# Last stage of a four-layer token tower: the weighted sum of gathered rows on VectorE in place of ScalarE and one reduction

## The reference

```
q = (x @ Wq).reshape(b, n, HEADS, DIM) * DIM ** (-0.5)
kv_scores, indices = _pk(x, Wq_pk, pk_keys)
offsets = jnp.arange(HEADS) * NUM_KV
ind = indices + offsets[None, None, :, None]
k = jnp.einsum('bnhk,bnhkd->bnhd', kv_scores, keys_table[ind])
v = jnp.einsum('bnhk,bnhkd->bnhd', kv_scores, values_table[ind])
sim = jnp.einsum('bihd,bjhd->bhij', q, k)
...
attn = jax.nn.softmax(sim, axis=-1)
out = jnp.einsum('bhij,bjhd->bhid', attn, v)
return out @ Wo
```

## Time and profile before

| what | us |
|---|---|
| median of three runs | 12374.88 |
| profiled execution, own time | 12427.32 |
| its span, first to last instruction | 12425.6 |
| PE busy | 9322.9 |
| DVE busy | 8840.9 |
| ACT busy | 6949.5 |
| POOL busy | 6941.6 |
| first gather of the last stage starts | 5385.5 |
| last maximum (L2966) starts | 12382.7 |

### The profile page before, as it was taken

How to read it: one execution, slowest core, us unless ns; L and a number is a source line. 1 busy time by engine, 2 the same in 40 slices (tenths; PEclk the granted TensorE clock), 3 DMA queues, 4 the chain that set the end, 5 groups by cost and what they waited for, 6 DMA issues and landing times.

```text
span 12425.6 us, 139805 instructions
## 1 busy us (share of the span) xinstructions
PE 9322.9 (75%) x38094; PEld 4917.2 (40%) x38094; DVE 8840.9 (71%) x23183; ACT 6949.5 (56%) x15135; POOL 6941.6 (56%) x5848
## 2 busy tenths in 40 slices
PE   1565667566745656359989989898999889898987
PEld 1251222222213113225545545454555445554545
DVE  3633899789983884777777777777777777777762
ACT  0211544354431002148777877788788778777784
POOL 3000777577750000057777777777777777777671
PEclk9955788778875777579999999999999999999996
DMA  0000333233320000022222222222222222222220
GB/s 20 8 17 3 113 119 124 82 116 119 126 75 11 14 7 9 1 58 64 60 65 60 67 57 63 59 63 59 61 64 58 64 56 65 58 64 60 61 58 19
DMA packets 538617, 723.65 MB, mean 58 GB/s; under 512 B 412866, under 2 KB 420593, under 8 KB 503386
## 3 DMA queue, kind: packets, MB, share of 16 engines
q0 software_dynamic: 168448, 338.54, 10.2%
q1 hardware_dynamic: 369418, 376.55, 9.8%
HBM read 697.87 MB, written 8.42 MB: 57 GB/s over the span
## 4 chain that ended last, share of the span: by engine, by line
PE 32%; DVE 10%; ACT 7%; issue 4%; DVEq 4%; ACTq 0%
PE l3m_acc L2580 7%; PE l3m_O L2551 6%; PE l3m_S L2535 4%; PE l3m_DX L2570 4%; PE l3m_T L2542 3%; PE l3m_S L2570 2%; ACT l3m_spread L2676 2%; DVEq L2883 2%; ACT l3m_prob L2707 2%; DVE l3m_hot L2885 1%; DVE l3m_nmax L2966 1%; PE l3m_DX L2571 1%; PE l3m_T L2500 1%; ACT l3m_probT L2716 1%; ACT l3m_W L2728 1%
## 5 line engine op out<-in xcount | busy, mean ns | idle before, releaser
L2475 POOL DMA_INDIRECT l3m_got<-in_l_table,l3m_row x5120 | 5029.8, 982 | 1843.6 <-issue 1079.1
L2676 ACT ACTIVATE l3m_spread<-l3m_got,l3m_weight 128x128 f32<-128x128 f32 x5120 | 2444.0, 503 | 19.6 <-DVE l3m_kv L2955 16.1
L2580 PE MATMUL l3m_acc<-l3m_W,l3m_values 128*128 128x512 f32 x3072 | 1675.9, 628 | 199.0 <-ACT l3m_W L2728 194.1
L1325 POOL TENSOR_TENSOR m_mul<-m_st,m_wide_c 128x2048 f32<-128x2048 f32 x256 | 1158.4, 4525 | 432.2 <-DVE m_st L1598 426.4
L2716 ACT ACTIVATE l3m_probT<-l3m_T 128x512 f32<-128x512 f32 (+3 forms) x1280 | 689.1, 538 | 626.0 <-PE l3m_T L2542 618.8
L1391 PE MATMUL m_W<-m_mul,tower_ident 128*128 128x512 f32 (+1 forms) x1536 | 807.7, 644 | 133.5 <-POOL m_mul L1325 78.0
L2551 PEld LDWEIGHTS l3m_O<-l3m_vo_g,l3m_probT 128*128 128x128 f32 x5440 | 733.5, 198 | 235.9 <-ACT l3m_probT L2716 171.8
L2542 PEld LDWEIGHTS l3m_T<-tower_ident,l3m_prob 128*128 128x128 f32 x4352 | 532.8, 149 | 680.9 <-issue 553.0
L2551 PE MATMUL l3m_O<-l3m_vo_g,l3m_probT 128*128 128x64 f32 x5440 | 749.5, 279 | 59.9 <-ACT l3m_probT L2716 59.9
L2707 ACT ACTIVATE l3m_prob<-l3m_S,l3m_nmax 128x1024 f32<-128x1024 f32 (+7 forms) x768 | 651.9, 854 | 251.6 <-DVE l3m_nmax L2966 251.4
L2542 PE MATMUL l3m_T<-tower_ident,l3m_prob 128*128 128x128 f32 x4352 | 757.8, 292 | 9.9 <-ACT l3m_vo_g L2697 5.7
(11 more groups left out here) (696 smaller groups left out, 19394.6 us busy)
## 6 DMA issues: line engine op xcount, KB each, us to landing
m_wide_c<-l1a_c SPq DMA_DIRECT2D x256, 1024.0 KB, 4.6
l3m_got<-in_l_table,l3m_row POOLq DMA_INDIRECT x5120
l3m_values<-in_l_table SPq DMA_DIRECT2D x288, 256.0 KB
l0i_img<-in_l_x SPq DMA_DIRECT2D x4, 1024.0 KB, 8.1
l2r_x<-l2a_hT SPq DMA_DIRECT2D x8, 512.0 KB, 5.4
qp_inw<-in_q_inw SPq DMA_DIRECT2D x1, 2336.0 KB, 8.1
l_kept<-l0t_xt,l0t_row POOLq DMA_INDIRECT x128, 2.2
l1a_c<-m_listf SPq DMA_DIRECT2D x16, 128.0 KB, 4.8
```

The lines of the kernel that those rows point to most:

```text
L1325: pool.tensor_tensor(mul[:, k % 2], st[:, k % 2], wide_c[:, k % CRING], ALU.mult).then_inc(multiplied, 1)
L2475: pool.indirect_dma_start(got[:, unit % GOT, j, :], None, table, bass.IndirectOffsetOnAxis(ap=row[:, unit // QUAD % RING, unit % QUAD, j:j ...
L2580: pe.matmul(acc[:], values[:, tile, :], W[:], start=(tile == 0), stop=(tile == TILES - 1)).then_inc(blended, 1)
L2676: copy = act.activation(spread[:, unit % 2, :, j], got[:, unit % GOT, j, :], ACT.Copy, scale=weight[:, g % RING, t, j:j + 1])
```

## The change

ACT's `part_up` and its calls go, and `spread` with them. DVE gets `add_rows`. Rows 0 to 3 of a unit each start one of four sums in `heap` (row times weight); rows 4 to 15 are multiplied by their weight and added to sum j % 4 by one instruction each. Behind row 15 the four sums are added as two pairs into `joined`, and the two into `kv`. DVE takes the rows of step s at four places of the step: 2 behind `scale`, 3 behind `top`, 3 behind `top_pairs`, the rest ahead of the second half of `rank` or `decode`. Each call drains first. POOL's wait on `parted` and PE's on `summed` now look to DVE; `shared` is gone, as weights and sums are on one engine.

```
-    def unit_summed(s):
-
-        ends = [j // TOPK for j in copies(s - 1) if j % TOPK == TOPK - 1]
-        return ends[0] if ends else None
...
-        got, spread = u.sb("got", [P, GOT, TOPK, KV]), u.sb("spread", [P, 2, KV, TOPK])
+        got, heap = u.sb("got", [P, GOT, TOPK, KV]), u.sb("heap", [P, 2, HEAPS, KV])
+        joined = u.sb("joined", [P, HEAPS // 2, KV])
...
-            def part_up(some):
-                for k in some:
...
-                    copy = act.activation(spread[:, unit % 2, :, j], got[:, unit % GOT, j, :], ACT.Copy,
-                                          scale=weight[:, g % RING, t, j:j + 1])
...
+            def add_rows(some):
+                if some:
+                    dve.drain()
+                for k in some:
+                    unit, j = k // TOPK, k % TOPK
+                    g, t = unit // QUAD, unit % QUAD
+                    if j == 0:
+                        dve.wait_ge(*arrived(unit))
+                    to, one = heap[:, unit % 2, j % HEAPS, :], weight[:, g % RING, t, j:j + 1]
+                    if j < HEAPS:
+                        dve.tensor_scalar(to, got[:, unit % GOT, j, :], one, None, ALU.mult).then_inc(parted, 1)
+                    else:
+                        dve.scalar_tensor_tensor(to, got[:, unit % GOT, j, :], one, to, ALU.mult,
+                                                 ALU.add).then_inc(parted, 1)
+                    if j == TOPK - 1:
+                        dve.drain()
+                        pile = heap[:, unit % 2]
+                        dve.tensor_tensor(joined[:], pile[:, 0:HEAPS // 2], pile[:, HEAPS // 2:], ALU.add)
+                        dve.drain()
+                        if t == 0 and g >= 3:
+                            dve.wait_ge(t_made, T_at["kv", "g", g - 3] + 1)
+                        halves = joined[:].rearrange("p i (s d) -> p i s d", s=2)
+                        out = kv[:, g % 3, t, :].rearrange("p (s d) -> p s d", s=2)
+                        dve.tensor_tensor(out[:, ::-1, :] if g % 2 else out, halves[:, 0], halves[:, 1],
+                                          ALU.add).then_inc(summed, 1)
...
+                mine = copies(s)
+                add_rows(mine[0:2])
...
+                add_rows(mine[2:5])
...
+                add_rows(mine[5:8])
...
-                unit = unit_summed(s)
-                if unit is not None:
-                    sum_up(unit)
+                add_rows(mine[8:])
```

More of the change, by code:

```diff
@@ L2159 @@
 COPIES = TOPK * GQ // QUADS
-GOT, RING, FREED, LATER = 4, 5, 1, 3
+GOT, RING, FREED, LATER, HEAPS = 4, 5, 1, 3, 4
 ABSENT = float(TOPK)
@@ L2414, in mix_heads @@
         picked, found, weighed = u.sem("picked"), u.sem("found"), u.sem("weighed")
-        shared, parted, summed = u.sem("shared"), u.sem("parted"), u.sem("summed")
+        parted, summed = u.sem("parted"), u.sem("summed")
         t_made, t_taken = u.sem("t_made"), u.sem("t_taken")
@@ L2665, in weigh @@
                 last.then_inc(weighed, 1)
-            def part_up(some):
-                for k in some:
-                    unit, j = k // TOPK, k % TOPK
-                    g, t = unit // QUAD, unit % QUAD
-                    if j == 0:
-                        act.wait_ge(shared, g + 1)
-                        if unit >= 2:
-                            act.wait_ge(summed, unit - 1)
-                        act.wait_ge(*arrived(unit))
-                    copy = act.activation(spread[:, unit % 2, :, j], got[:, unit % GOT, j, :], ACT.Copy,
-                                          scale=weight[:, g % RING, t, j:j + 1])
-                    if j % FREED == FREED - 1:
-                        copy.then_inc(parted, 1)
             def take_q(kind, g, slot):
@@ L2774, in _ @@
                 n, todo = tile_at(s), pieces(s)
-                mine = list(copies(s))
-                share = -(-max(len(mine) - 1, 0) // (3 * turns(s))) if turns(s) else len(mine)
-                def some_up(mine=mine, share=share):
-                    part_up(mine[:share])
-                    del mine[:share]
                 coming = tile_at(s + 1)
@@ L2786, in _ @@
                     take_O(tile_at(s - 1))
-                part_up(mine[:1])
-                del mine[:1]
                 if coming is not None and turns(s) == 0:
@@ L2793, in _ @@
                         take_flip(n, c)
-                    some_up()
                     if c < len(todo):
                         grow(todo[c])
-                    some_up()
                     ahead = c + 1 < len(todo) and other(todo[c + 1])
@@ L2804, in _ @@
                         take_extra(use, (s + 2 - QUAD * LAG) // QUAD % 2)
-                    some_up()
                     if c + 1 < len(todo) and not ahead:
                         lift(todo[c + 1])
-                part_up(mine)
                 p, t = pick_at(s - 1)
@@ L2946, in share @@
                 dve.tensor_tensor(weight[:, g % RING], weight[:, g % RING], bc(total[:, p % 2, :], TOPK),
-                                  ALU.mult).then_inc(shared, 1)
-            def sum_up(unit):
-                g, t = unit // QUAD, unit % QUAD
-                if t == 0 and g >= 3:
-                    dve.wait_ge(t_made, T_at["kv", "g", g - 3] + 1)
-                dve.wait_ge(parted, copies_done(unit, TOPK))
-                out = kv[:, g % 3, t, :].rearrange("p (s d) -> p s d", s=2)
-                dve.tensor_reduce(out[:, ::-1, :] if g % 2 else out, spread[:, unit % 2].rearrange(
-                    "p (s d) j -> p s d j", s=2), AX, ALU.add).then_inc(summed, 1)
+                                  ALU.mult)
+            def add_rows(some):
[23 more added lines that the diff above has]
+                                          ALU.add).then_inc(summed, 1)
             def peak(n):
```

## The result

| kernel | median us | lowest to highest | ratio to before, 95% interval |
|---|---|---|---|
| before | 12375.4 | 12367.07 to 12380.56 | |
| changed | 12674.99 | 12667.41 to 12695.85 | 1.0245 (1.0228 to 1.0263) |

A forecast was written before the change was run, and what follows sets the result against it. PE and ACT were taken to bound most steps, DVE the heavy ones. DVE's added 1095 us exceeded 972 us of waits by 123; with 40 unfilled, +25 ahead and -8 in the tail, +180 us: 12550 us, range 12340 to 12800.

The forecast's parts named there:

- B: Rival, chance 0.12: gathers become the bound, held up by adds reading two SBUF tensors; 1.39 us a row, 12680 us.
- C: Rival, chance 0.14: DVE cannot shift its work into its waits, a quarter of 972 us is left; 12760 us.
- Term (1): ACT loses 10 copies of 503 ns a step; at most the 227 us they held on the chain come back.
- (2): Starting a sum on DVE, a 128-wide TENSOR_SCALAR: 1210 at 0.196 us of spacing, 237 us.
- (3): Adding a row on DVE, SCALAR_TENSOR_TENSOR: 3630 at 0.27 us of spacing, 980 us (710 to 1270).
- (5): Joining the four sums of a unit on DVE: 0.94 us for each of 302 units, 284 us.
- Term (4): New drains on DVE ahead of `add_rows` calls: three a step at 0.16 us, 232 us.
- Term (7): Friction of DVE's new sum starts with POOL's gathers: 40 ns for each of 1210, 48 us.
- The spare time, 972 us: DVE's five long waits in the 484 steps, 2.0 us a step, taken as its whole spare time for new work.
- I leave 40 us unfilled: Estimate of the part of DVE's waits that new work cannot fill: 4% of 972 us, between 0 and 243.
- Start and tail: Outside the 484 steps: +25 us on DVE ahead of them, -8 us in the tail's 17 steps that still copy.
- A: Rival, chance 0.22: faster, as DVE does not fill if an added row is spaced under 0.236 us; 12245 us.

The follow-up runs named there:

- e3: The changed kernel without the gathers of odd rows from the fifth unit on, DVE's work kept: 12672.49 us, ratio 1.0222.
- e8: The changed kernel with ACT's ten scaled copies a step put back, of a constant tile into an unread buffer: 12733.59 us, ratio 1.0273.
- e9: The kernel before with `store` (second place or later) and the subtraction into `tail` moved to the end of DVE's step: 12189.16 us, ratio 0.9834.
- e5: The changed kernel with `store` (second place or later) and the subtraction into `tail` moved to the end of DVE's step: 12571.81 us, ratio 1.0133.
- e1: The changed kernel without a unit's multiply-adds and joins, one scaled row passed on as the sum, all gathers kept: 12121.64 us, ratio 0.9781.
- e10: e9 with `share`, the reciprocals of the weights' sums, also moved behind `store` and `tail`: 12209.49 us, ratio 0.9851.
- e7: The kernel before with DVE scaling the last 8 of a unit's 16 rows, ACT the others, reduction kept: 12595.97 us, ratio 1.0159.
- e4: The changed kernel with all ten rows of a step taken at one place, behind `scale`, in calls of four rows: 12639.69 us, ratio 1.0189.

## Why the prediction was right, and where it was off

The sign, the bound (DVE ends last) and the range held: 12675 us lies in 12340 to 12800, slower by 2.4%. Within it the forecast of 12550 us was 120 us low, beyond the 12470 to 12640 of its own mechanism. That band varied the spacing of an added row, which came out as forecast, and not the waits that stay, for which the text itself gave 0 to 243 us.

That the range held is in part luck of its width: it also took in B and C. The number alone would have pointed to B (12680 us), whose mechanism e3 refutes. Of the forecast's own signs, DVE's share (85% of the window, forecast 86% or more), ACT's wait for the maxima (615 us), the spacing of the adds and the length of the gathers came out or nearly so. Two did not: ACT's busy time, and the waits. Those for `stage` and `tail` are 128.5 + 76.2 = 205 us, and over 200 us was the sign of rival C.

- **Term (1), ACT's copies.** Nearly nothing came back, as said; e8 puts it at 35 us. But ACT is busy 3614 us and not 2720. Going by 0.503 us a copy was wrong for busy time: the copies overlap with their neighbours. In e9 two in a row take 0.79 us together, so the second adds 0.29 us, and the drop of 1539 us is 0.32 us for each of 4840. The chain's 227 us was an upper bound that says little.
- **Terms (2), (3), (5), the instructions.** Right. Three adds in a row take 0.89 us, one 0.346 in the median: spacing 0.27 us, as forecast from the 256-wide pair. Three starts take 0.68 us, one 0.285: 0.20 us for 0.196. The rows, in one step with two of the joins:

```profile
8602.81 0.62 DVE L2930 SCALAR_TENSOR_TENSOR l3m_heap<-l3m_got,l3m_weight,l3m_heap 128x128 f32<-128x128 f32 x2
8603.53 0.42 DVE L2935 TENSOR_TENSOR l3m_joined<-l3m_heap 128x256 f32<-128x256 f32 x1
8604.03 0.29 DVE L2941 TENSOR_TENSOR l3m_kv<-l3m_joined 128x128 f32<-128x128 f32 x1
...
8606.20 0.68 DVE L2928 TENSOR_SCALAR l3m_heap<-l3m_got,l3m_weight 128x128 f32<-128x128 f32 x3
...
8623.34 0.89 DVE L2930 SCALAR_TENSOR_TENSOR l3m_heap<-l3m_got,l3m_weight,l3m_heap 128x128 f32<-128x128 f32 x3
```

  The Trainium skill (VectorE: DVE Perf Modes, section on the TRN2 errata) would have 0.19 us where 0.27 us was measured. The measurement decides; by its figure the term would have been 280 us too small.
- **Term (4), drains.** DVE's short gaps rose by 195 us, from 609 to 804 (window less busy less the long waits). The forecast's 232 us held the lost overlap too, and the whole tells more: DVE's need went from 6480 - 972 = 5508 to 6769 - 217 = 6552 us, +1044 for the 1095 of the sum.
- **Term (7), friction.** A gather's mean is 990 ns for 983 (forecast: at most 50 ns more); a start took 303 ns in the mean at a median of 285, up to 529, so 18 ns of friction for the 40 of the forecast.
- **The spare time, 972 us, and "I leave 40 us unfilled".** This is the step of the prediction that failed. 217 us stayed, not 40, within the bound of a quarter (243) that was given. With it the window adds up, as it must when need and waits make it up: 1044 - 972 + 217 = +289 us, measured +290. The reason given was that what DVE waits for has long been done when DVE is late. That is so for the exponent sums, whose waits went. It isn't so for `store` and `tail`, which depend on PE and ACT. That these two are late because DVE's own maxima were late is a likely reading, since ACT stands 615 us for maxima; no run separates it from PE and ACT being simply not through yet. e5 shows the price: with the two behind the rest of the step's work the waits fell by 140 us and the window by 134.
- **Start and tail.** +16 and -13 us for +25 and -8.

Rivals. A fell with its condition: adds are spaced 0.27 us, not under 0.236. Its cap by POOL's rate (6286 us) was about right and is reached elsewhere, in the windows of e1 (6229) and e9 (6270). B fell by e3, and by its own sign: POOL's waits for DVE to free the ring did not vanish (653 + 194 us) and DVE waits for no landed row; gathers grew by 7 ns, not 100. C (12760 us) had the right mechanism, and its price for the waits (243) was nearer than the forecast's 40. It is 85 us too high: its three terms were each above what was measured (1095 for 1044, 243 for 217, and 17 for 3 at start and tail). Its reason, that heavy picks and deep tiles fall in different steps, is only half of it: by the table, the dense steps and the "g" steps without the decode are the ones that got more work than they had waits (1.94 for 1.04 and 2.12 for 1.70 us), while the waits were in the steps with the decode (5.84 us), and the sum over all hid it.

## What to carry to other kernels

Before the waits of an engine are counted as room for more work, split them by the kind of step in which they stand and compare need and waits in each kind; a sum over all steps is room only if work can cross from one kind to the other. And look at what is queued behind each wait: a wait in the middle of an engine's list, with work that needs no waiting and the loop's next hand-over (here the row maximum) behind it, can be lost time. Moving the two waiting instructions behind that work, to just ahead of the hand-over, was worth 1.7% here, without moving any work between engines. A third one moved in the same way (e10) brought nothing.

## What the runs showed of the hardware

- **Indirect gathers have a rate of their own.** A gather of one row of 128 values for each of 128 partitions takes 0.94 us in the median, 0.98 in the mean, and the next starts 0.30 us after its end when nothing holds it: 1.28 to 1.29 us a row. In e1 and e9 such rows fill the whole window. The mean of one in the windows of the other runs with all gathers is 0.98 to 1.01 us (the most in e7).
- **A two-input DVE instruction and the gathers hardly collide when short.** The forecast's rival B was built on one 1.23 us instruction that held up a gather by 0.4 us. With 3628 adds of 0.35 us in the window, the mean gather grew by 7 ns, and halving the gathers took 21 us off DVE's busy time in e3. Even the 7 ns can't be put down to the adds: in e9, without them, the mean gather is 990 ns too, and in e4, with them, 983. The Trainium skill (SBUF — State Buffer, section Who interferes with whom) has the second of the two wait for the whole of the first; these runs show little of it for instructions this short: at most 7 ns a gather, where rival B had 100.
- **TensorE's granted clock was lower where it stood more, in these three windows.** The same 28,000 or so matmuls, at a mean granted clock of 0.96, kept PE busy 5840 us before; at 0.94, with PE's loads standing 955 us for the exponentials in place of 715, 5948 us; at 0.98 in e9, where they stood 568.5 us, 5753 us. It is no strict order: e3 has 0.93 with 914.5 us of such standing. A mean under 1 means that part of the stage ran at the lower of the two levels, 1.2 in place of 2.4 GHz. The 108 us that PE's busy time gained lie beside the 290 us of the window; how much of these they account for was not separated.
